# A graph network in one kernel: the third layer's attention logits as four products into quarters of one PSUM bank

## What is computed

```python
xl = (x @ W_l + b_l).reshape(-1, H, O)
xr = (x @ W_r + b_r).reshape(-1, H, O)
ee = (edge_attr @ W_e).reshape(-1, H, O)
m = jax.nn.leaky_relu(xl[src] + xr[dst] + ee, NEG_SLOPE)
logits = jnp.einsum('eho,ho->eh', m, att)
lmax = jax.ops.segment_max(logits, dst, num_segments=N)
exl = jnp.exp(logits - lmax[dst])
denom = jax.ops.segment_sum(exl, dst, num_segments=N)
alpha = exl / (denom[dst] + 1e-16)
msg = xl[src] * alpha[:, :, None]
out = jax.ops.segment_sum(msg, dst, num_segments=N)
return out.reshape(-1, H * O) + b_att
```

## Time and profile before

| | us |
|---|---|
| median of 3 runs | 7552.22 |
| lowest, highest | 7548.44, 7554.6 |
| span of the profiled execution | 5796.6 |
| TensorE busy | 4596.1 |
| GpSimd busy | 3988.9 |
| VectorE busy | 2702.8 |
| ScalarE busy | 1216.6 |

### The profile page before, as it was taken

One profiled execution on the slowest core, in us unless ns is written; L12 is line 12 of the kernel. 1 busy time (PEld: TensorE's weight loads), 2 busy tenths in 40 slices (PEclk: granted clock), 3 DMA queues, 4 the chain that ended last, 5 costly groups with the idle time before them and its releaser, 6 DMA issues. The chain is left out here.

```text
span 5796.6 us, 89863 instructions
## 1 busy us (share of the span) xinstructions
PE 4596.1 (79%) x21959; PEld 3153.3 (54%) x21959; DVE 2702.8 (47%) x8105; ACT 1216.6 (21%) x3182; POOL 3988.9 (69%) x4207
## 2 busy tenths in 40 slices
PE   5888888657777776999999977687777758887887
PEld 4777777535556564444444433455555535555555
DVE  4222222321111113677777766555555545555555
ACT  2111111221211211222222258111111111111111
POOL 6777777457777775777777700777777747777775
PEclk9999999975555555999999989666666666666665
DMA  5333333244444443555555510455555534444443
GB/s 151 106 105 105 105 104 104 74 150 106 112 114 107 118 114 90 160 165 165 165 165 164 166 38 24 109 114 114 113 114 115 113 77 107 111 109 110 109 111 78
DMA packets 559823, 663.58 MB, mean 114 GB/s; under 512 B 196431, under 2 KB 390909, under 8 KB 558717
## 3 DMA queue, kind: packets, MB, share of 16 engines
q1 hardware_dynamic: 424909, 382.99, 22.2%
q0 software_dynamic: 134640, 277.80, 21.1%
HBM read 580.95 MB, written 86.19 MB: 115 GB/s over the span
## 5 line engine op out<-in xcount | busy, mean ns | idle before, releaser
L1792 POOL DMA_INDIRECT soft_rows<-table,sources x2496 | 2388.6, 957 | 1128.2 <-issue 737.7
L1422 POOL DMA_INDIRECT sum_rows<-table,sources x832 | 785.7, 944 | 343.9 <-issue 249.6
L1088 POOL DMA_INDIRECT term_rows<-table,sources x832 | 791.4, 951 | 289.4 <-issue 289.4
L1923 PE MATMUL psum<-soft_onehot,soft_message 128*128 128x64 f32 x3328 | 647.6, 358 | 107.1 <-DVE soft_message L2066 105.0
L1923 PEld LDWEIGHTS psum<-soft_onehot,soft_message 128*128 128x128 f32 x3328 | 586.1, 266 | 188.0 <-issue 181.8
L1119 PE MATMUL psum<-term_onehot,term_term 128*128 128x64 f32 x1664 | 403.9, 425 | 188.5 <-DVE sums L1171 176.6
L1464 PE MATMUL psum<-sum_onehot,sum_rows 128*128 128x64 f32 x1664 | 360.4, 391 | 222.7 <-DMA sum_rows<-table,sources 218.4
L1119 PEld LDWEIGHTS psum<-term_onehot,term_term 128*128 128x128 f32 x1664 | 370.7, 328 | 242.1 <-issue 242.0
L1165 DVE TENSOR_TENSOR term_term<-psum,term_rows 128x512 f32<-128x512 f32 x208 | 143.9, 692 | 753.0 <-issue 349.0
L1464 PEld LDWEIGHTS psum<-sum_onehot,sum_rows 128*128 128x128 f32 x1664 | 343.5, 304 | 278.0 <-issue 273.8
L1919 PEld LDWEIGHTS psum<-soft_onehot,soft_weights 128*4 128x4 f32 (+1 forms) x3328 | 284.9, 109 | 305.9 <-issue 293.0
(11 more groups left out here) (277 smaller groups left out, 6619.9 us busy)
## 6 DMA issues: line engine op xcount, KB each, us to landing
soft_onehotT<-onehotsT SPq DMA_DIRECT2D x312, 256.0 KB
soft_onehot<-onehots SPq DMA_DIRECT2D x624, 128.0 KB, 2.1
soft_attrs<-in_ea128T SPq DMA_DIRECT2D x208, 256.0 KB
soft_rows<-table,sources POOLq DMA_INDIRECT x2496
term_attrs<-in_ea64T SPq DMA_DIRECT2D x208, 128.0 KB, 2.8
onehots<-term_onehot SPq DMA_DIRECT2D x208, 128.0 KB
sum_onehot<-onehots SPq DMA_DIRECT2D x208, 128.0 KB, 2.7
onehotsT<-sum_flat SPq DMA_DIRECT2D x208, 128.0 KB
```

What stands on the lines that cost most here:

```text
L1088: pool.indirect_dma_start(rows[:, k, t, :], None, io.table0[0:NCH * CN], bass.IndirectOffsetOnAxis(sb.sources[:, g * TPG + t:g * TPG + t + ...
L1422: pool.indirect_dma_start(rows[:, k, t, :], None, io.table1[0:NCH * CN], bass.IndirectOffsetOnAxis(sb.sources[:, g * TPG + t:g * TPG + t + ...
L1792: pool.indirect_dma_start(rows[:, k, t, :], None, table[0:NCH * CN], bass.IndirectOffsetOnAxis(sb.sources[:, g * TPG + t:g * TPG + t + 1], ...
L1923: last = pe.matmul(bank[:, 0:W], message[:, g.slot(4), b, :], onehot[:, k, b], start=b == 0, stop=b == TPG - 1)
```

## The change

`soft_sweep` is split. Layers 4 and 5 keep it without the branches for `full`; their instructions stay the same. Layer 3 gets `gatv2_sweep`:

- `head_logits` runs once a batch, at the start of the step after the batch's last group. It makes four products with one and the same 128 x 32 matrix `att_cols` (8 columns used, 24 zero) from the four groups' `z` into partitions 0 to 31, 32 to 63, 64 to 95 and 96 to 127 of one bank. None adds to another. The lanes are now group x 32 + head, in 128 partitions of which 32 are used.
- `z` has four buffers instead of two, the lane bank one instead of two; `starts`, `cont`, `lanes` and the rest have 128 partitions.
- `starts` and `cont` are loaded by four DMAs each, eight partitions apiece, and cleared once.
- The weights go back to edge order by four products with `quad_pick`, a 128 x 32 one-hot matrix, in place of four transposes.
- The backward scan stands after the edge sum in VectorE's queue, and ScalarE's copy of the lanes ahead of the exponential.
- The first phase loads four constants in place of one.

```diff
                 def head_logits(g):
-                    j = g.slot(BATCH)
-                    pe.wait_ge(s.leaky, g.times(1, 1))
-                    if j == 0 and g.back(2 * BATCH).exists():
-                        pe.wait_ge(s.shifted, g.back(2 * BATCH).uses(BATCH))
-                    pe.matmul(lane_bank[g.half()], sb.att8[:, j], z[:, g.slot(2)], start=j == 0, stop=j == BATCH - 1).then_inc(s.logits, 1)
+                    pe.wait_ge(s.leaky, g.times(1, BATCH))
+                    if g.back(BATCH).exists():
+                        pe.wait_ge(s.factor_log, g.back(BATCH).uses(BATCH))
+                    settle(pe)
+                    for j in range(BATCH):
+                        last = pe.matmul(lane_bank[j * QUAD:(j + 1) * QUAD], sb.att_cols, z[:, j], start=True, stop=True)
+                    last.then_inc(s.logits, 1)
...
                 def step(t):
+                    if t.back(BATCH).closes(0):
+                        head_logits(t.back(BATCH))
                     if t.exists():
-                        (edge_terms if full else dst_logits)(t)
+                        edge_terms(t)
...
                     g = t.back(LAG)
                     if g.exists():
-                        (scatter if full else scatter_T)(g)
-                    if full and t.back(1).exists():
-                        head_logits(t.back(1))
-                    if g.exists() and full:
-                        flip_window(g)
+                        scatter(g)
+                        flip_window(g)
...
                         for b in range(TPG):
-                            last = pe.transpose(weights_bank[:, b * L:(b + 1) * L], lanes[:, piece(b)], sb.ident[0:L, 0:L])
+                            last = pe.matmul(weights_bank[:, b * L:(b + 1) * L], lanes[:, piece(b)], sb.quad_pick, start=True, stop=True)
...
-                    sp.dma_start(starts[:, 0:GE], io.lane_starts[bass.ds(g.batch(), 1), 0:L].rearrange("a l e -> (a l) e")).then_inc(s.starts_in, 16)
+                    for j in range(BATCH):
+                        sp.dma_start(starts[j * QUAD:j * QUAD + H, 0:GE], lanes_of(io.lane_starts, g, j)).then_inc(s.starts_in, 16)
...
+                v.memset(starts, 0.0).then_inc(s.cleared, 1)
+                v.memset(cont, 0.0).then_inc(s.cleared, 1)
```

More of the change, by code:

```diff
@@ L42 @@
 BATCH = 4
+QUAD = P // BATCH
 LAG = BATCH + 3
@@ L1659, in soft_sweep @@
+    spread = {3: sb.lane_expand4, 4: sb.ones}[layer]
     mask, heads = sb.lane_mask[0:L], sb.lane_head[0:L, 0:H]
     AHEAD = 4
-    DST = AHEAD if full else BATCH
     phase = f"soft{layer}"
-    FIRST = AROUND if full else 4 * AROUND
-    LAST = G + LAG if full else STEPS * (NCH - 1 + BEHIND) + 14
-    names = ("order cleared starts_in cont_in rows_T rows_out edge_term z leaky src_out logits lanes_out running backward fend carry_psum carry shift init_psum init maxima "
-             "shifted factor_log weights_lane factor spread weights_T weights_out factor_psum factor_out columns message "
-             "scattered window_copied window_T").split()
@@ L1668, in soft_sweep @@
-    s = sems(nc, phase, *names, gathered=AROUND, attr=AHEAD, dst_rows=DST, onehotT=4, onehot=4)
+    FIRST = 4 * AROUND
+    LAST = STEPS * (NCH - 1 + BEHIND) + 14
+    names = ("order cleared starts_in cont_in edge_term leaky src_out logits lanes_out running backward fend carry_psum carry shift init_psum init maxima "
+             "shifted factor_log weights_lane factor spread weights_T weights_out factor_psum factor_out message "
+             "scattered").split()
+    s = sems(nc, phase, *names, gathered=AROUND, dst_rows=BATCH, onehotT=4, onehot=4)
@@ L1711, in soft_sweep @@
         factor_head_bank = sb.psum[0:H, 7, 48:48 + BATCH]
-        nodes = None if full else GatNodes(nc, io, sb, tile, layer, sb.psum[:, 2, :])
-        CLEARED = 4 + (not full)
+        nodes = GatNodes(nc, io, sb, tile, layer, sb.psum[:, 2, :])
+        CLEARED = 5
         ORDER = 4
@@ L1809, in step @@
                 def step(t):
-                    if not full and t.back(BATCH).closes(0):
+                    if t.back(BATCH).closes(0):
                         take_sources(t.back(BATCH))
@@ L1846, in step @@
                     if g.closes(0):
-                        act.wait_ge(s.logits, g.times(1, BATCH) if full else g.uses(BATCH))
+                        act.wait_ge(s.logits, g.uses(BATCH))
                         if g.back(BATCH).exists():
@@ L1899, in src_logits @@
                     last.then_inc(s.logits, 1)
-                def scatter(g):
-                    k = g.slot(4)
-                    wait_past(pe, s.window_copied, g, 1, 0)
-                    pe.wait_ge(s.onehot[k], g.uses(4, 16))
-                    pe.wait_ge(s.columns, g.times(1, 1))
-                    pe.wait_ge(s.message, g.times(1, 1))
-                    for b in range(TPG):
-                        last = pe.matmul(window_bank, onehot[:, k, b], message[:, g.slot(2), b, :], start=b == 0, stop=b == TPG - 1)
-                    last.then_inc(s.scattered, 1)
                 def scatter_T(g):
@@ L2011, in add @@
                     v.tensor_scalar(heads_first, heads_first, factor_head[:, q, j:j + 1], None, ALU.mult).then_inc(s.order, 1)
-                    v.wait_ge(s.window_T if full else s.scattered, g.times(1, 1))
+                    v.wait_ge(s.scattered, g.times(1, 1))
                     bank = window_T[g.slot(2)]
@@ L2021, in running_max @@
                     n = g.uses(BATCH)
-                    logits, highest = lane_bank[g.half()], running_bank[g.half()]
+                    logits, highest = lane_bank[g.half()], running_bank
                     v.wait_ge(s.lanes_out, n)
-                    if not full:
-                        v.scalar_tensor_tensor(logits, logits, 0.2, lanes, ALU.mult, ALU.max).then_inc(s.leaky, 1)
-                        v.wait_ge(s.leaky, n)
+                    v.scalar_tensor_tensor(logits, logits, 0.2, lanes, ALU.mult, ALU.max).then_inc(s.leaky, 1)
+                    v.wait_ge(s.leaky, n)
                     v.wait_ge(s.starts_in, g.uses(BATCH, 16))
@@ L2071, in step @@
                 def step(t):
-                    g = t.back(1)
-                    if g.exists() and full:
-                        v.wait_ge(s.z, g.times(1, 1))
-                        v.scalar_tensor_tensor(z[:, g.slot(2)], z[:, g.slot(2)], 0.2, z[:, g.slot(2)], ALU.mult, ALU.max).then_inc(s.leaky, 1)
                     g = t.back(LAG)
```

468 lines of the change are left out of this document (359 added, 109 removed).

## The result

The changed kernel takes 7604.14 us (median of 13 runs, 7559.55 to 7615.83) beside 7554.6 us of the kernel before in the same comparison (13 runs, 7543.2 to 7574.96). The ratio is 1.0056, with a 95% interval from 1.0043 to 1.007: slower, by some 42 us (the two medians are 49.5 apart). The forecast was 7636, slower by 84. The sign is right and the size is twice too large. The way there was wrong in two large terms that happened to cancel in part, which is luck, and on other ground they don't cancel.

The account below looks back on a forecast made before the run. TensorE was taken to bound the layer-3 sweep at 20.55 us a batch. The change made it 19.69 plus 2.45, or 22.14; over 52 batches, with clearings, 84 us more: 7636 us, range 7545 to 7735.

Parts of the forecast that it names:

- The sum without L: Layer-3 sweep, TensorE per batch: 20.55 us with removals, waits and growth counted, before the four side-by-side logits products: 19.69 us.
- L: Time per batch of the four side-by-side logits products on TensorE: 2.45 us, taking only neighbouring records to overlap.
- the window wait: After each scatter, TensorE's window transposes wait for ScalarE's window copy: 0.50 us a step, 2.00 a batch.
- the wait for the exponentials: TensorE waits at L1963 for the VectorE and ScalarE chain: 0.72 instead of 0.24 us, plus 0.48 a batch.
- the weights' products: Four real one-hot products returning weights to edge order: 1.00 us against 0.42 for transposes, plus 0.58 a batch.
- the eight loads and the clearings: Loads of starts and cont on SP's queue, issued ahead, no cost; clearings before VectorE's first sum, 0.9 us once.
- VectorE's leaky step: Last group's step on VectorE before the new logits: z ready at about 2.6 us, TensorE there at 2.88, no wait.
- rival A: Logits products overlap fully: 0.98 us together, batch 20.67, plus 7 us, total 7559; chance 0.24.
- rival C: TensorE's idle pieces lower its clock; one group's L1873 and L1874 per batch at half clock, plus 94 us, 7730; chance 0.13.
- The 1755.6 us: Difference between the 5796.6 us profiled span and the 7552.22 us median, taken as unaffected time around the span.
- The cap by GpSimd: GpSimd's sixteen gathers a batch take 20.0 to 20.56 us, capping TensorE gains beyond roughly 0.3 us per batch.
- rival D: Full overlap of the logits products and eight short records at 0.42 us: batch 20.09, total 7529; chance 0.10.

## Why the prediction was right, and where it was not

**The sum without L (19.69) nearly held.** At full clock a batch of the changed kernel takes 20.8 us, and L is 1.00: 19.8 without it. With the products one after the other it is 23.7 - 3.54 = 20.2, half a microsecond over the forecast, which I can't place. Its terms: the window wait was 0.50 a step and is 1.69 - 1.07 = 0.62; the wait for the exponentials was to be 0.72 and is 0.60; the weights' products were to take 1.00 and take 0.88 (L1881 2846.72 to L1885 2847.60). The work of VectorE, the eight loads and the clearings show no cost that I can find. VectorE's leaky step, put at nothing, costs 13 us of waits ahead of L1834 in the whole sweep, 0.25 a batch.

**L was mis-sized: 2.45 forecast, 1.00 measured.** The step that failed is that the second record of a product holds back the next product's first. It does not. Eight records take what two take. That was rival A's L. It cost 1.45 x 52 = 75 us of the 84. The Trainium skill, "TensorE: Matmul & The Clock Gate", Part 3, says that products in different column strips run at the same time; the trace agrees, with 1.00 against 3.54 us for the same four products on the whole width. I had that statement beside an objection that no row bore out, and took the objection.

**The clock was the cause, and I gave it 0.13.** With L right and the clock full, the change comes to rival A: 20.69 a batch, +7 us, no difference. Nearly everything beyond is rival C. I priced it at 94 us for one pair of groups a batch. On smooth ground it is 6.4 us in 39 batches of 51 and makes nearly all of the 270 us; on the ground of the result the clock goes from 0.84 to 0.74 and the groups that no edit touches grow by 102.6 us. No run filled the waits there, so on that ground the clock's part rests on the profiles alone. My reason against it, that piled-up work makes TensorE dense again, was wrong: the half clock lasts 13.7 us in the median fall and comes back in most batches. That the forecast came out near the result is the sum of an L that was too large and a clock that was left out, and so luck.

**The 1755.6 us.** I carried them over as time around the span. They are in it. The step ran from one profiled execution to the median of others without asking whether they were alike. The consequence is in the result: where late signals already keep TensorE waiting and its clock at 0.84, the change has less clock to take away, which is my reading of why it costs 42 us and not 270; no run tests it by itself.

**The cap by GpSimd** (20.0 to 20.5 a batch) is borne out as far as the runs go: with transposes, steady batches don't get under 20.3 (those of before: 20.2), though TensorE idles in them. So rival D had no room. What I overlooked is that on smooth ground GpSimd is not next but first. Its gathers in the sweep of the kernel before and of the changed one (busy, mean ns | idle before):

```profile
L1792 POOL DMA_INDIRECT soft_rows<-table,sources x794 | 778.2, 980 | 242.1 <-issue 238.2 <-DVE soft_message L2066 4.0
L1766 POOL DMA_INDIRECT soft_rows<-table,sources x793 | 757.1, 955 | 499.8 <-DVE soft_message L1974 303.6 <-issue 196.3
```

Before, only 4.0 of 1072 us are a wait for the messages that free its buffers: the gathers follow one another, and their 20.56 us a batch are the batch. After, that wait is 303.6 us, and TensorE sets the pace.

The range, 7545 to 7735, holds 7604, and on the ground where its rows were taken the same working would have given 5804 (A) to 5975 (C), and a range of 5789 to 5979, against 6074: outside.

Of the versions tried on both grounds none is clearly better than the kernel before on both: transposes for the weights gives 0.9981 on one and 1.0076 on the other.

## What to carry to other kernels

Before you remove work that stands between a producer and its reader on TensorE, look at what that work covered. Short uncovered waits add little to the sum, but here the clock halved around the step that had two of them, beside eight short products, in 39 of 51 batches, and that cost was many times the waits. Compare the profiled span with the timed median first, and if they differ by more than a few per cent, profile again until you have an execution of the timed kind.

## What the hardware showed that I had not expected

- Four f32 products in different quarters of the columns, two records each, take 1.00 us together, as long as one alone (0.98).
- The kernel can be made faster by products that nobody needs: 832 records in the waits, 183 us less (clock 0.96 against 0.79). With transposes for the weights, where the clock stood at 0.96 without them, they were worth nothing clear of the noise.
- The same program on the same data takes 5804 or 7550 us, by the comparison it is in. In the longer kind what TensorE signals can arrive up to 5.8 us late (6.5 with the window transposes one step later), in about one step of four in the kernel before and one of six in the changed one; which step, and how often, depends on the order of work. What decides between the kinds (the chip, for one), and what makes the signals late, stays open.
